# Newton step and scale of the group norm moved from VectorE to ScalarE, two edge rows written by one activation

## The reference

```
g = v.reshape(B_, G, C_ // G, H_, W_)
m = jnp.mean(g, axis=(2, 3, 4), keepdims=True)
s = jnp.var(g, axis=(2, 3, 4), keepdims=True)
gn = ((g - m) / jnp.sqrt(s + eps)).reshape(v.shape)
wq = _quantize(weight, Wp, Wn)          # Wp * (1 or 0), -Wn * (1 or 0)
x = x + conv3x3(gn, wq, padding 1) + bias
```

## Time and profile before

| | |
|---|---|
| median of 3 runs | 574.85 us (574.74 to 574.89) |
| profiled execution, its own time | 575.64 us |
| span of its instructions | 574.0 us |
| granted TensorE clock, mean | 0.989 of full |
| busy: PE / DVE / ACT / POOL | 534.1 / 542.9 / 504.4 / 166.2 us |
| the same as shares | 93% / 95% / 88% / 29% |

### The profile page before, as it was taken

How to read it: one execution, slowest core, us unless ns; L and a number is a source line. 1 busy time by engine, 2 the same in 40 slices (tenths; PEclk the granted TensorE clock), 3 DMA queues, 4 the chain that set the end, 5 groups by cost and what they waited for, 6 DMA issues and landing times.

```text
span 574.0 us, 9367 instructions
## 1 busy us (share of the span) xinstructions
PE 534.1 (93%) x3238; PEld 320.1 (56%) x3238; DVE 542.9 (95%) x506; ACT 504.4 (88%) x485; POOL 166.2 (29%) x107
## 2 busy tenths in 40 slices
PE   0597999999999999999999999999999999999994
PEld 0453555555555555555555555565555555555552
DVE  1986999999999999999999999999999999999994
ACT  3588999999999999999999999999999999999850
POOL 2203312333332223333222333332233333212330
PEclk9997999999999999999999999999999999999998
DMA  8433999999999999999999999999999999998767
GB/s 297 192 113 87 257 280 271 301 288 248 316 263 299 311 297 259 314 302 286 273 272 293 294 288 293 303 294 272 288 310 274 286 295 308 274 282 200 160 181 271
DMA packets 28104, 153.43 MB, mean 267 GB/s; under 512 B 3504, under 2 KB 3504, under 8 KB 28080
## 3 DMA queue, kind: packets, MB, share of 16 engines
q1 hardware_dynamic: 18576, 102.77, 47.1%
q0 software_dynamic: 8928, 49.78, 44.9%
q10 hardware_dynamic: 576, 0.59, 0.3%
HBM read 101.75 MB, written 51.38 MB: 267 GB/s over the span
## 4 chain that ended last, share of the span: by engine, by line
DVE 68%; issue 24%; PE 4%; DMA 2%; DVEq 1%; ACT 1%; ACTq 0%
DVE parts L581 25%; DVE y L600 18%; DVE plane L541 10%; DVE plane L547 10%; DMA y<-in_L_conv_weight_dram 2%; PE even_rows L732 2%; DVE newton L570 2%; PE odd_rows L732 1%; DVEq L157 1%; DVE plane L553 1%; DVE neg_var L559 1%; ACT parts L386 1%; DVE rstd L565 0%; PE even_rows L697 0%; DVE parts L587 0%
## 5 line engine op out<-in xcount | busy, mean ns | idle before, releaser
L732 PE MATMUL odd_rows<-parts,w_lhsT 128*128 128x385 f16 (+1 forms) x1536 | 266.8, 330 | 8.6 <-DVE parts L581 7.5
L732 PE MATMUL even_rows<-parts,w_lhsT 128*128 128x385 f16 (+1 forms) x1536 | 267.6, 331 | 3.7 <-DVE parts L587 2.9
L581 DVE SCALAR_TENSOR_TENSOR parts<-plane,norm_scale,parts 128x1568 f16<-128x1568 f32 x127 | 233.4, 1842 | 4.3 <-ACT parts L386 4.3
L324 POOL TENSOR_TENSOR plane<-x 128x1512 f32<-128x1512 f32 x32 | 109.2, 3413 | 384.1 <-DVE parts L581 366.9
L732 PEld LDWEIGHTS even_rows<-parts,w_lhsT 128*128 128x128 f16 x1536 | 150.0, 98 | 111.9 <-issue 8.7
L732 PEld LDWEIGHTS odd_rows<-parts,w_lhsT 128*128 128x128 f16 x1536 | 148.1, 100 | 108.2 <-DVE parts L581 9.4
L386 ACT ACTIVATE parts<-plane,norm_scale 128x1568 f16<-128x1568 f32 x127 | 199.8, 1597 | 9.8 <-ACT plane L426 5.2
L432 ACT ACTIVATE junk<-x,negmean 128x3136 f16<-128x3136 f32 x32 | 92.9, 2904 | 0.0
L392 ACT ACTIVATE junk<-x 128x3136 f16<-128x3136 f32 x31 | 86.9, 2804 | 0.0
L600 DVE SCALAR_TENSOR_TENSOR y<-even_rows,out_scale,d_sb 128x784 f32<-128x784 f32 x62 | 61.0, 1025 | 0.0
L600 DVE SCALAR_TENSOR_TENSOR y<-odd_rows,out_scale,c_sb 128x784 f32<-128x784 f32 x62 | 60.9, 1023 | 0.0
(11 more groups left out here) (65 smaller groups left out, 127.2 us busy)
## 6 DMA issues: line engine op xcount, KB each, us to landing
x<-in_x_dram SPq DMA_DIRECT2D x64, 784.0 KB, 11.7
out_dram<-y SPq DMA_DIRECT2D x63, 784.0 KB, 5.7
y<-in_x_dram POOLq DMA_DIRECT2D x62, 784.0 KB, 11.8
out_dram<-y SPq DMA_DIRECT2D x2, 392.0 KB, 6.2
y<-in_L_conv_weight_dram ACTq DMA_DIRECT2D x1, 576.0 KB, 10.7
wp_sb<-in_L_conv_Wp_dram ACTq DMA_DIRECT2D x1, 0.5 KB, 6.3
wn_sb<-in_L_conv_Wn_dram ACTq DMA_DIRECT2D x1, 0.5 KB, 7.9
bias_sb<-in_L_conv_bias_dram ACTq DMA_DIRECT2D x1, 0.5 KB, 12.2
```

What stands on the lines that cost most here:

```text
L324: nc.gpsimd.tensor_tensor(plane[B][:, 0:PAIRS - 1, :], even[:, 0:PAIRS - 1, :], even[:, 1:, :], ALU.subtract).then_inc(plane_ready[B], 1)
L581: nc.vector.scalar_tensor_tensor(part(img, j, LO), plane[j][:], norm_scale[:, b_slice(img)], part(img, j, HI), ALU.mult, ALU.subtract).the ...
L732: ins = nc.tensor.matmul(product_ps(odd, b, b + 1)[:, 0, :, to:to + n], w_lhsT[:, prod, kw, :], part(img, prod, which)[:, b * BANK_ROWS:(b ...
```

## The change

`newton_factor` and `scale_of_x` leave DVE. A new `scale_of_x` on ACT does the same arithmetic in three activations on 128 x 1: the square of rstd0, the square times neg_var plus 3, and that times rstd0. Each waits for the one before by a semaphore. DVE keeps the reciprocal. The four planes become slices of one tensor, so that one activation with a stride can write both edge rows.

```diff
-        plane = [sb(f"plane{j}", [P, PAIRS, W]) for j in range(4)]
+        planes = sb("planes", [P, 4, PAIRS, W])
+        plane = [planes[:, j] for j in range(4)]
...
-                    xs, bias = x_sb[img.buf], negmean[:, b_slice(img)]
-                    nc.scalar.activation(plane[A][:, 0, :], xs[:, 1, :], ACT.Identity, bias=bias)
-                    nc.scalar.activation(plane[B][:, PAIRS - 1, :], xs[:, H - 2, :], ACT.Identity,
-                                         bias=bias).then_inc(edges_ready, 1)
+                    first, last = A * PAIRS, B * PAIRS + PAIRS - 1
+                    rows = planes[:].rearrange("p j r w -> p (j r) w")[:, first:last + 1:last - first, :]
+                    nc.scalar.activation(rows, x_sb[img.buf][:, 1:H - 1:H - 3, :], ACT.Identity,
+                                         bias=negmean[:, b_slice(img)]).then_inc(edges_ready, 1)
...
+                def scale_of_x(img):
+
+                    b = b_slice(img)
+                    act.wait_ge(rstd_ready, img.count(plus=1))
+                    nc.scalar.activation(rstd_sq[:, b], rstd0[:, b], ACT.Copy, scale=rstd0[:, b]).then_inc(rstd_sq_ready, 1)
+                    act.wait_ge(rstd_sq_ready, img.count(plus=1))
+                    nc.scalar.activation(newton[:, b], rstd_sq[:, b], ACT.Identity, bias=three[:, 0:1],
+                                         scale=neg_var[:, b]).then_inc(newton_ready, 1)
+                    act.wait_ge(newton_ready, img.count(plus=1))
+                    nc.scalar.activation(norm_scale[:, b], newton[:, b], ACT.Copy,
+                                         scale=rstd0[:, b]).then_inc(scale_of_x_ready, 1)
...
                         root(nxt)
+                        scale_of_x(nxt)
                         make_first_hi(nxt)
...
                             sum_x(far)
+                        if nxt and not second_slot:
+                            scale_of_x(nxt)
                         copy_d(now)
                         if second_slot:
                             root(nxt)
                             sum_x(far)
+                            scale_of_x(nxt)
...
+            nc.vector.memset(three[:], 3.0)
...
-                def newton_factor(img):
-                    b = b_slice(img)
-                    dve.wait_ge(rstd_ready, img.count(plus=1))
-                    nc.vector.tensor_scalar(newton[:, b], rstd0[:, b], rstd0[:, b], neg_var[:, b],
-                                            ALU.mult, ALU.mult).then_inc(newton_ready, 1)
-
-                def scale_of_x(img):
-                    b = b_slice(img)
-                    dve.wait_ge(newton_ready, img.count(plus=1))
-                    nc.vector.tensor_scalar(norm_scale[:, b], newton[:, b], 3.0, rstd0[:, b],
-                                            ALU.add, ALU.mult).then_inc(scale_of_x_ready, 1)
```

More of the change, by code:

```diff
@@ L88, in conv_preact_kernel @@
         rstd0 = sb("rstd0", [P, X_BUFS])
+        rstd_sq = sb("rstd_sq", [P, X_BUFS])
         newton = sb("newton", [P, X_BUFS])
+        three = sb("three", [P, 1])
         norm_scale = sb("norm_scale", [P, X_BUFS])
@@ L134, in conv_preact_kernel @@
         rstd_ready = sem("rstd_ready")
+        rstd_sq_ready = sem("rstd_sq_ready")
         newton_ready = sem("newton_ready")
@@ L632, in emit @@
                         first_rstd(nxt)
-                        newton_factor(nxt)
-                        scale_of_x(nxt)
                         turned_weights((B,))
```

## The result

The changed kernel takes 584.78 us (median of 4 runs, 584.50 to 585.46) against 574.81: 9.97 us more, ratio 1.0175, 95% interval 1.0158 to 1.0193. The forecast was 583.0, range 577.5 to 593.0.

The account below looks back on a forecast made before the run. The prediction took DVE, full at 16.61 us a slot, as the bound before, and a 16.86 us ring over ACT and DVE after; 30 x 0.25 plus 0.66 adds 8.2 us, giving 583.0 us, range 577.5 to 593.

Parts of the forecast that it names:

- The ring: Closed path from DVE's reciprocal over ACT's three activations, copy D and hi C, then lo C to the next reciprocal: 16.86 us.
- The engine-by-engine rival: Middle slots: the fullest engine alone sets the slot, ACT at 16.47 us, giving 571.3 us; chance almost nothing.
- The price of the line: ACT, from the first of the three new activations to the start of copy D: 0.92 us, between 0.55 and 1.25.
- the long waits of the upper end: ACT waiting on itself between the new activations: 0.20 us per wait at most; rival with 0.17 each, 591.4 us, chance 0.16.
- The short activations: Rival: the three new activations on ACT cost 0.55 us, giving 571.5 us; faster by one of two rivals, chance 0.11.
- DVE's wait: DVE in front of lo C waits 0.81 us for ACT in every slot, more than the 0.56 saved.
- DVE's step behind the reciprocal: Without the two tiny instructions, DVE's lo B follows the reciprocal after 0.07 us instead of 0.63.
- Product B: PE in the middle slot: copy D ends at 15.33 us after lo C, PE ends A at 15.41, so not late.
- The edge rows: One ACT activation of 0.38 us for two saves 0.19 us per slot, which does not count in the ring.
- The sum: Whole kernel: 30 slots at 0.25 us give 7.5, plus 0.66 at the start and second slot, 8.2 us slower.
- the start: Opening slot: DVE starts plane D 0.56 us sooner, so hi D starts at 25.69 instead of 26.08, 0.39 us sooner.
- The clock: Rival: PE drops to its lower clock, over 60 us in all; chance 0.05 together with a cost in between.

## Why the prediction was right

**The ring** was right in form and nearly in size: 16.90 us for 16.86. Adding to the line on ACT costs its full length, adding to DVE or taking from ACT outside the ring does nothing, and taking copy D or plane D out of the ring by order alone removes the loss. The engine-by-engine rival, which said 571.3 from ACT's 16.47, was wrong for the changed kernel; the one with the earlier reciprocal (571.16, slot 16.44) shows it.

**The price of the line** was 0.95 us for 0.92. The square and the last product took 0.295 us for 0.29, and the wait on the own engine was 0.03 to 0.04, as in the earlier trace rows; the long waits of the upper end stayed where they had been, behind the edge rows. The middle activation took 0.387 for 0.36: its second operand from memory added 0.09 to the first, where I had taken 0.17 for two from a PSUM row. The Trainium skill, "ScalarE: Activation LUTs", section on what ACT_TABLE_LOAD costs, gives about 93 ns for each, and this trace agrees (0.387 - 0.295 = 0.092). The short activations fell with it: the 224 cycles for ScalarE of "VectorE: DVE Perf Modes" (the Trainium skill, section on the TRN2 errata) leave out 0.1 us for each operand from memory.

**DVE's wait** ahead of lo C was 0.76 for 0.81, ACT's ahead of the square 0.34 for 0.4, and DVE's step behind the reciprocal 0.07, as put. Product B came some 0.2 us late, where the prediction had it in time: the tiny product ahead of it starts at 301.57, 0.24 us behind the end of copy D, and A's 24 matmuls started at 297.39 and need 3.99. PE had the time to spare. It then went from B to C without the wait that the prediction saw there.

**The edge rows** gained 0.18 to 0.19 us a slot on ACT, 0.38 us for the one activation, and nothing in time, as put.

**The sum** came out 1.8 us short: 8.2 for 9.97. In the profiled runs, which are 9.82 apart, lo C of the last image is 556.30 - 546.57 = 9.73 us later; what follows explains that part, and the last 0.2 us between it and the medians is not traced. Of the difference to 8.2, about 1.0 is the slot, 0.28 for 0.25 over 30 slots, mostly the middle activation. The other 0.5 is the start: the 0.39 us that I had DVE's plane D bring never came. Plane D started sooner and ended when it had, since it ran beside GpSimd's plane B:

```profile
20.96 3.39 POOL L328 TENSOR_TENSOR planes<-x 128x1512 f32<-128x1512 f32 x1 [17.25 <-DVE planes L562]
...
23.30 2.70 DVE L568 TENSOR_TENSOR planes<-x 128x1568 f32<-128x1568 f32 x1
...
26.09 1.60 ACT L390 ACTIVATE parts<-planes,norm_scale 128x1568 f16<-128x1568 f32 x1 [0.26 <-DVE planes L568]
```

Its 2.14 in the earlier trace rows beside 1.78 in the slots was the sign of this, and I took it for the price of the instruction. The remaining 0.14 is the second slot, whose product C on PE took 6.32 us for 6.19, at a mean granted clock of 0.65 for 0.66. **The clock** otherwise stayed, 0.988 for 0.989, and 24 matmuls 4.15 us.

## What to carry to other kernels

When engines hand work round, the slot is the longest closed path through their lists. One engine's own list is such a path, and a path over several can be longer than the fullest of them. Moving an instruction to an engine with room lengthens the slot if it lands between a hand-over and the work that waits for it. Here its place was worth as much as its price: the same instructions in another order gave 10.0 and 13.6 us, and one activation more cost 10.8. Before moving work, look for where the new wait will stand, and move what is queued in front of the result (here the reciprocal's one step) along with it. Idle time ahead of a wait is no room for work behind it.

## What the hardware showed

- GpSimd's tensor_tensor and DVE shut each other out where DVE's instruction reads two tensors from SBUF. A one-column tensor_tensor on GpSimd took 0.19 us beside an idle DVE and 3.36 us beside lo B and plane A, ending as they ended; the other way round, beside a GpSimd instruction that had begun first, DVE's plane D took 2.70 us for 1.78, and its one-column square 1.45 for 0.16. Where plane B of the first image met two half-size lo parts, both lost: 4.08 us for 3.41, and 5.13 for 1.97. Whoever is running finishes first. GpSimd was let in behind DVE's plane D and plane A, and not between lo B and plane A. The Trainium skill, "GPSIMD Engine Reference", section on key points, says that the two share their SBUF interfaces and conflict where a DVE instruction has two inputs in SBUF; these runs agree and put 3.36 us for 0.19 on it.
- DVE instructions with one tensor from SBUF, or with one of two in PSUM, were not held. In the kernel before, the reciprocal and the first of the Newton pair ran beside the same plane B at their usual length:

```profile
20.93 3.41 POOL L324 TENSOR_TENSOR plane<-x 128x1512 f32<-128x1512 f32 x1 [17.22 <-DVE plane L541]
...
22.94 0.27 DVE L570 TENSOR_SCALAR newton<-rstd,neg_var 128x1 f32<-128x1 f32 x1
```

- In the slots plane B costs nothing: its 3.41 us lie beside DVE's output pieces, which read one operand from PSUM. Two pieces take 1.97 us there, and 1.98 at the end of the run with no GpSimd work beside them.
- An activation on one column that reads SBUF took 0.19 us with no scale or bias from memory, 0.295 with one and 0.387 with two. Behind one of its own engine that it waits for it started 0.03 to 0.04 us after that one's end, but hi A started 0.17 to 0.20 us behind the edge rows. What makes that difference was not tried.
